# Emulated GRU steps: where the state's turn, the picks and the row loads stand

## The reference, cut to what matters

```python
def cell(h, x):
    gi = x @ W_ih + b_ih                      # 64x512 @ 512x1536
    gh = h @ W_hh + b_hh
    i_r, i_z, i_n = jnp.split(gi, 3, axis=-1)
    h_r, h_z, h_n = jnp.split(gh, 3, axis=-1)
    r = jax.nn.sigmoid(i_r + h_r)
    z = jax.nn.sigmoid(i_z + h_z)
    n = jnp.tanh(i_n + r * h_n)
    h_new = (1.0 - z) * n + z * h
    return (h_new, h_new)
...
_, hs = jax.lax.scan(cell, initial_state, jnp.swapaxes(inputs, 0, 1))
```

## Time and profile before

| | us |
|---|---|
| runs | 2875.29, 2875.74, 2877.38 (median 2875.74) |
| span of the profiled execution | 2879.2 |
| time of the profiled execution beside its span | none is given apart from it |
| PE busy | 2562.9 |
| ACT busy | 1140.6 |
| DVE busy | 1685.2 |
| POOL busy | 1262.3 |

### The profile page before, as it was taken

One profiled execution on the slowest core, in us unless ns is written; L12 is line 12 of the kernel. 1 busy time (PEld: TensorE's weight loads), 2 busy tenths in 40 slices (PEclk: granted clock), 3 DMA queues, 4 the chain that ended last, 5 costly groups with the idle time before them and its releaser, 6 DMA issues. The chain is left out here.

```text
span 2879.2 us, 154632 instructions
## 1 busy us (share of the span) xinstructions
PE 2562.9 (89%) x67605; PEld 1681.0 (58%) x67605; DVE 1685.2 (59%) x3398; ACT 1140.6 (40%) x2317; POOL 1262.3 (44%) x598
## 2 busy tenths in 40 slices
PE   2088999998889999999999999999996999999995
PEld 1066777776768888887675564655642444444442
DVE  8852222225632222225646778867592888888887
ACT  1321222225632222224702333323232777777773
POOL 0255666662046666664061363622700333333334
PEclk8599999999999999999999999999998999999998
DMA  6833222224422222226554253442432223232322
GB/s 193 239 85 77 74 73 71 73 71 112 131 63 71 74 73 70 73 71 167 152 135 127 92 151 118 115 156 85 129 143 93 74 84 95 84 95 84 95 63 53
DMA packets 234843, 293.74 MB, mean 102 GB/s; under 512 B 69581, under 2 KB 194023, under 8 KB 233895
## 3 DMA queue, kind: packets, MB, share of 16 engines
q1 hardware_dynamic: 212743, 240.84, 30.6%
q10 hardware_dynamic: 18304, 36.19, 3.6%
q0 software_dynamic: 3680, 15.21, 1.9%
HBM read 231.61 MB, written 60.45 MB: 101 GB/s over the span
## 5 line engine op out<-in xcount | busy, mean ns | idle before, releaser
L1145 PE MATMUL psum<-second_shared 64*32 64x384 f16 x32768 | 1026.0, 324 | 50.2 <-issue 31.3
L1153 PE MATMUL psum<-low_w,low_hot 64*32 64x384 f16 x16384 | 756.5, 324 | 2.0 <-issue 2.0
L1372 DVE TENSOR_SCALAR second_shared<-psum 32x384 f16<-32x384 f32 x496 | 272.3, 549 | 749.1 <-PE psum L1145 741.9
L953 POOL TENSOR_TENSOR low_hot<-first_shared,sum_mask 128x1024 f16<-128x1024 f16 x256 | 499.8, 1952 | 430.1 <-DVE first_shared L1359 183.8
L1145 PEld LDWEIGHTS psum<-second_shared 64*32 64x32 f16 x32768 | 561.5, 93 | 198.0 <-issue 89.8
L947 POOL TENSOR_TENSOR second_shared<-first_shared,whole_mask 128x2048 f16<-128x2048 f16 x128 | 462.5, 3614 | 460.1 <-PE psum L1145 348.2
L1044 ACT ACTIVATE second_shared<-psum 32x384 f16<-32x384 f32 x496 | 239.8, 483 | 801.9 <-PE psum L1145 795.9
L1233 PE MATMUL psum<-low_w,low_hot 64*64 64x384 f16 x12288 | 513.7, 326 | 19.9 <-issue 13.5
L1233 PEld LDWEIGHTS psum<-low_w,low_hot 64*64 64x64 f16 x12288 | 378.3, 108 | 150.4 <-issue 18.4
L310 PE MATMUL psum<-w_x,x_cols 128*64 128x512 f32 (+1 forms) x1856 | 312.0, 495 | 9.5 <-ACT x_cols L280 9.5
L1153 PEld LDWEIGHTS psum<-low_w,low_hot 64*32 64x32 f16 x16384 | 282.5, 93 | 56.8 <-issue 3.1
(11 more groups left out here) (286 smaller groups left out, 2746.6 us busy)
## 6 DMA issues: line engine op xcount, KB each, us to landing
low_w<-w_rows SPq DMA_DIRECT2D x384, 144.0 KB
low_w<-w_rows SPq DMA_DIRECT2D x256, 120.0 KB
second_shared<-w_rows SPq DMA_DIRECT2D x1024, 24.0 KB, 1.9
x_gates<-x_out ACTq DMA_DIRECT2D x58, 384.0 KB, 2.3
xg<-x_gates SPq DMA_DIRECT2D x58, 384.0 KB, 3.2
low_w<-w_rows SPq DMA_DIRECT2D x256, 72.0 KB
low_w<-w_rows SPq DMA_DIRECT2D x384, 48.0 KB
w_rows<-quantised SPq DMA_DIRECT2D x24, 384.0 KB, 4.9
```

What stands on the lines that cost most here:

```text
L953: nc.gpsimd.tensor_tensor(low_hot[:, buf].rearrange("p (s k) b -> p s k b", s=SUBS), low_a[:, slot, bass.ds(c, 1), :, :].rearrange("p a s ...
L1145: last = nc.tensor.matmul(run[m][u][j * Q:(j + 1) * Q, :], whole_hot[rows[u], m, sign, kk, j % 2 * Q:(j % 2 + 1) * Q], whole_w[rows[u], m, ...
L1153: nc.tensor.matmul(run[m][u][j * Q:(j + 1) * Q, :], low_hot[rows[u], m, kk, j % 2 * Q:(j % 2 + 1) * Q], low_w[rows[u], m, at:at + UC], sta ...
L1372: last = nc.vector.tensor_scalar(whole_w[u * B:u * B + Q, m, 0, bq, :], run[m][u][bq * Q:(bq + 1) * Q, :], 1.0 / HIGH_ONE, None, ALU.mult)
```

## The change

1. `turn(t + 1)` moves ahead. For states 1 and 2 it stands behind block 28 of chain (2,0) and (3,0); for states 3 to 5 it stands between the last two steps of the window before (`behind_first`). DVE's `cut_state` of states 1 and 2 moves ahead of the gates of the x chain.
2. Of the picks of steps 2 to 5, three stay ahead of the chain; the others stand behind block 0 (three) and block 1 (two). The first eight blocks of these chains, and the last four of the x chains, are written out instead of looped over. The picks' banks are taken in the order 6, 4, 5, and PE's wait for the window's last taking out moves from the window's end to between pick 0 and pick 1.
3. SP issues the x rows of step 1 one transfer behind each block's weights of chain (2,0), from block 4 on.
4. At a window's start PE turns the first rows ahead of the clears, and ACT copies them ahead of the biases and no longer waits for the step's gates.
5. ACT's wait for the end of the pair chain ahead of chain (3,0) goes, and the loads of `w_x` move behind the one-hots of that chain.

```diff
-            def load_low(eng, operand, kinds, slot):
+            def low_rows(eng, operand, kinds, slot):
                 for r, kind in enumerate(kinds):
                     for u in range(2):
                         at = u * B + r * SK
                         eng.dma_start(low_a[at:at + SK, slot]..., pieces[operand, kind]).then_inc(rows_of_in[slot], 16)
+                        yield
...
+            def low_then_whole(eng, operand, m, slot):
+                yield from low_rows(eng, operand, LOW_ROWS, slot)
+                yield from whole_rows(eng, operand, m, slot)
...
-            def x_pairs(pe, pairs, w, banks):
+            def x_pairs(pe, pairs, w, banks, behind_first=None):
+                turn_rows(pe, pairs[0], banks)
                 for rz, new in banks[1]:
...
                 last.then_inc(x_cleared, 1)
-                turn_rows(pe, pairs[0], banks)
                 for j in pairs:
                     x_step(pe, 2 * j, w, banks)
                     if j + 1 in pairs:
                         turn_rows(pe, j + 1, banks)
+                    elif behind_first:
+                        behind_first()
                     x_step(pe, 2 * j + 1, w, banks)
-                pe.wait_ge(x_out_ok, 2 * pairs[-1] + 2)
...
-                SEL_BANKS = (4, 5, 6)
+                SEL_BANKS = (6, 4, 5)
...
-                        for c in range(4 * BUFS):
+                        next_rows = low_then_whole(sp, 1, 0, ROWS_X0)
+                        for c in range(NBK):
                             load(2, 0, c, sum_buf(c))
-                            if c == 2 * BUFS - 1:
+                            if c == BUFS:
                                 sp.wait_ge(hot_ok, block_no(2, 0, 0) + 1)
-                                load_low(sp, 1, LOW_ROWS, ROWS_X0)
-                        load_whole(sp, 1, 0, ROWS_X0)
-                        sum_blocks(sp, sum_load(2, 0), 4 * BUFS, 4 * BUFS)
+                            if c >= BUFS:
+                                next(next_rows, None)
...
                             a.wait_ge(gates_ok[0], 2 * X_SUMS)
-                            a.wait_ge(gates_ok[1], 2 * (t + 1))
+                            copy_rows(a, pairs[0], WINDOW_BANKS)
                             a.wait_ge(x_cleared, t - FINE + 1)
                             place_bias(steps[0], WINDOW_BANKS)
                             place_bias(steps[1], WINDOW_BANKS)
-                            copy_rows(a, pairs[0], WINDOW_BANKS)
...
-                        a.wait_ge(run_ok[1], block_no(3, 0, 0) + BUFS)
+                        x_one_hots(3)
                         for k in range(KD):
                             a.dma_start(w_x[:, k, :], w_ih[k * P:(k + 1) * P, :]).then_inc(w_x_in, 16)
-                        x_one_hots(3)
...
-                        def sum_chain(t, m):
+                        def sum_chain(t, m, behind=None):
...
+                                    if behind and isinstance(n, int):
+                                        behind(n * BUFS + j)
...
+                            if m == 0:
+                                with pe.Fori(0, FOURS - 1) as n:
+                                    four(n, 0)
+                                four(FOURS - 1, 0)
+                                return
+                            for n in range(2):
+                                four(n, 0)
...
-                        def pick(t):
+                        def pick(t, first=0, last_one=None):
...
-                            x_pairs(pe, window_of(t), w_x, WINDOW_BANKS)
+                            x_pairs(pe, window_of(t), w_x, WINDOW_BANKS, (lambda: turn(t + 1)) if t + 1 < EXACT else None)
+
+                        def turn_behind(t, block):
+                            return lambda c: turn(t) if c == block else None
+
+                        def picks_behind(t):
+                            def behind(c):
+                                if c * SELS + SELS < places(t):
+                                    pick(t, (c + 1) * SELS, min((c + 2) * SELS, places(t)))
+                            return behind
...
-                            sum_chain(t + FINE, 0)
+                            sum_chain(t + FINE, 0, turn_behind(t + 1, NBK - BUFS))
                         for t in range(FINE, EXACT):
-                            turn(t)
                             pe.wait_ge(gates_ok[1], t * 2)
                             clear(t, 1)
-                            pick(t)
-                            sum_chain(t, 1)
+                            pick(t, 0, 1)
+                            if t > FINE:
+                                pe.wait_ge(x_out_ok, 2 * window_of(t - 1)[-1] + 2)
+                            pick(t, 1, SELS)
+                            sum_chain(t, 1, picks_behind(t))
                             x_window(t)
+                        pe.wait_ge(x_out_ok, 2 * X_PAIRS)
...
                             finish(elementwise(t))
+                            cut_state(t + 1)
                             gate_values(t + FINE, 0)
                         for t in range(FINE, EXACT):
-                            cut_state(t)
+                            if t > FINE:
+                                cut_state(t)
                             place_second(t)
```

More of the change, by code:

```diff
@@ L248, in load_low, with whole_rows @@
                                       pieces[operand, kind]).then_inc(rows_of_in[slot], 16)
-            def load_whole(eng, operand, m, slot):
+                        yield
+            def whole_rows(eng, operand, m, slot):
                 for u in range(2):
@@ L257, in load_whole, with load_low @@
                                           pieces[operand, kind].rearrange("k (c s) b -> s k c b", s=SUBS)[sub]).then_inc(rows_of_in[slot], 16)
+                            yield
+            def low_then_whole(eng, operand, m, slot):
+                yield from low_rows(eng, operand, LOW_ROWS, slot)
+                yield from whole_rows(eng, operand, m, slot)
+            def load_low(eng, operand, kinds, slot):
+                for _ in low_rows(eng, operand, kinds, slot):
+                    pass
+            def load_whole(eng, operand, m, slot):
+                for _ in whole_rows(eng, operand, m, slot):
+                    pass
             def x_banks(rows, *gates):
@@ L1236, in four @@
                                                 last.then_inc(run_ok[u], 1)
+                                    if behind and isinstance(n, int):
+                                        behind(n * BUFS + j)
                             FOURS = NBK // BUFS
                             tiles = TILES_OF.get(t, ()) if m == 1 else ()
+                            if m == 0:
[5 more added lines that the diff above has]
+                                four(n, 0)
                             if not tiles:
-                                with pe.Fori(0, FOURS) as n:
+                                with pe.Fori(2, FOURS) as n:
                                     four(n, 0)
                                 return
-                            with pe.Fori(0, 2) as n:
-                                four(n, 0)
                             if tiles[0] < KI:
@@ L1271, in turn @@
                             last.then_inc(turned, 1)
-                        def pick(t):
+                        def pick(t, first=0, last_one=None):
                             pe.wait_ge(cut_h, CUTS * t)
-                            for n in range(places(t)):
+                            for n in range(first, places(t) if last_one is None else last_one):
                                 group, whole = pick_of(t, n)
```

## The result

The changed kernel takes 2845.46 us (median; 2841.68 to 2848.57 in four runs) beside 2876.56 for the kernel before: a ratio of 0.9884, 95% interval 0.9867 to 0.9901. It is faster by about 33 us by the ratio (31 between the medians), where 54 were forecast, and lies 5 us above the range. The profiled execution spans 2842.2 us (2879.2 before); the forecast for it was 2825.0.

The account below looks back on a forecast made before the run. TensorE, busy in nine tenths of the span, was taken as the bound. Gains of 11.3, 8.3, 8.0, 5.7, 12.2, 0.7 and 8.0 sum to 54.2 us, taking 2875.74 to 2821.5; range 2808 to 2840.

Parts of the forecast that it names:

- Chain (2,0): First sum chain: one row load behind each block's weights lets it run without stands; gain 11.3 us, bounds 1.8 and 11.9.
- the turn of state 1: From the first sum chain to the pair chain's start: cut hidden under blocks, picks faster; gain 8.3 us (7 to 9.5).
- Chain (3,0): Second sum chain: without ACT's wait it takes 84.7 us from clears to turn, not 92.7; gain 8.0 (5.0 to 8.9).
- the rival of the bytes: w_x's moved loads meet step 2's index loads and first weights; price at most 9.0 us, time 2830.5; chance 0.10.
- Steps 3 and 4: Seams from last x matmul to sum chain: 14.9 us becomes 8.4, less 0.44 for the turn; gain 6.1 each, 12.2 together.
- the first rival: DVE becomes the bound in steps 3 and 4 too; both keep 1.3 us instead of 6.1, time 2831; chance 0.13.
- The picks' own time: Pick matmuls in the seams of steps 2 to 5: at full clock 30 in 3.00 us, 64 in 6.4.
- Step 2: Seam between chain (3,0) and step 2's chain, which begins as if after 8.4 us; gain 5.7, bounds 4.1 and 7.5.
- Step 5: DVE's tiles set the chain's pace, so the seam's gain is given back; 0.7 us remains, bounds -3 and +6.1.
- Windows: Four x windows: earlier copies and first steps back at full clock, less waits for the state; gain 8.0 us (0 to 9.2).
- the rival of the lower clock: Windows stay at the lower clock if a 1.5 us wait suffices; 4 x 1.5 lost, time 2827.5; chance 0.05.
- Straight code: Rival: 40 written-out blocks are fed too slowly; at 2 us more per block the time is 2901, slower; chance 0.03.

## Why the prediction was right and wrong

**Chain (2,0) and the turn of state 1** were right, alone (10.3) and together (18.6 of 19.6). What the chain lacks is short stands, 0.38 for ACT's one-hots and 0.68 with no releaser.

**Chain (3,0)**: ACT's wait went as said. What failed is "The loads of w_x, moved behind the last one-hot, are wanted some 100 us later": true, but their 3 MB met the index loads and the end of the chain. This is the rival of the bytes, given 0.10 and at most 9.0, worth 4.6. By the rule of the Trainium skill quoted there ("DMA: Bandwidth & Descriptors", section "Issuing engines are not separate DMA queues") the move only shifts the collision, and this trace agrees: 0.93 of wait for weights went at the chain's start, 3.14 came at its end. Whether weights or PE's instructions came late there is open; with the loads of w_x spread, the stand lies within the last block, where the program has no wait.

**The second pair chain** was "left alone by this change". Its code was, its start was not: 4.9 us behind a burst of loads on SP instead of 15.0, and the diff doesn't touch that burst. 4.3 lost, and no rival had it.

**Steps 3 and 4** are the step that failed most, 11.1 us. The lead was right: 2.2 forecast, 1619.84 - 1617.52 = 2.3 measured. Wrong was "after it both go round in 11 us". DVE's first rounds took 11.2, then 14.1 and 14.0, against PE's 11.07. In the kernel before, DVE waits for PE in each round from the second on (0.20 at the same operation), so I read as DVE's round what was PE's. Yet its first round showed more than 11: the second tile's values came 13.0 us behind the first's (1643.38 + 0.69 in the earlier trace rows), with only that 0.20 of wait in between, at the end of

```profile
1654.82 2.28 DVE L1423 SCALAR_TENSOR_TENSOR second_shared<-second_shared 128x512 f16<-128x512 bf16 x1
```

That was the first rival, given 0.13 and priced at 9.6. The forecast also priced the split picks at a gain on PE; measured, they cost 1.9 a step there and let DVE begin its tiles some 7 us later than with all picks ahead.

**The picks' own time** was too low in all four steps. The 30 matmuls in 3.00 us include those that only reach into the stretch: 64 take 7.15, not 6.4, though any stretch of 3.00 us within them shows 30. So the chains began as if 9.2 to 9.3 us behind the clears, where 8.4 was forecast. Step 2's 6.2 for 5.7 is therefore luck: its seam gave 4.9, and 1.3 came from shorter stands inside its chain, which no term had.

**Step 5** lost less than thought (3.0 gained for 0.7): three stands came, but only one slow four of blocks. **Windows**: right, 7.9 of 8.0. The first step takes 5.38, at a granted clock of 1.00 over 1511 to 1517, so a stand of 1.7 costs no clock, and the rival of the lower clock falls. The rule of the Trainium skill ("TensorE: Matmul & The Clock Gate", section "Loop structure matters more than you think"), taken for any wait, does not hold at this length. The turn waits at most 0.49 for the state. **Straight code**: written-out blocks run at 2.62, so that rival falls as it was put; but the sign set for it, a gap without a releaser inside them, did show, at the end of chain (3,0), where loads were under way.

With 11.1, 4.6 and 4.3 lost, and 2.3 more gained in step 5, most of the 17 us between the forecast and the profiled execution has its place. The range allowed for two of the losses together; three came. Left open is why chain (2,0) is cleared anywhere from 685.3 to 690.3 in these executions, 5 us beside spreads of 4 to 11 among the runs of one kernel.

## What to carry to other kernels

An engine that waits a little for another in every round shows the other's pace, not its own: before counting on slack, add up its operations in a stretch where it runs free. When a chain starts earlier, look at what the queues are doing at its new start, the fetch of its code included, though the edit touches none of it. And try the parts of an edit one by one: here the early turn was worth 33 us once the collisions were out of its way, the spread rows 10, and the split of the picks cost 15.

## What was not expected of the hardware

An operation of DVE takes 0.69 or 2.27 us by whether one of POOL's of 1.9 is under way, and the phase between the two repeats: 0.67 to 0.68 and 2.74 in both steps of all five executions that have the split picks and turn the tiles at their first place. PE stopped for 2.9 to 4.6 us inside a group of matmuls when a burst of loads (16 of 64 KB) was under way, always behind the same 135 matmuls; that its code came late is the likely reading. And the clock: the stand of 2.74 in step 3 left the next four blocks at 12.27 (granted clock 0.87 over 1668 to 1681), the same stand in step 4 of the same execution left none slower (1.00 over 1851 to 1862), and of step 5's stands of 2.41, 2.41 and 2.47 only the first left a slower four.
